# A macaron layer with routed experts on one core: dispatching two tiles at a time, with the norm's inverse deviation computed on the vector engine

## The reference

```python
x = x + 0.5 * ffn(layernorm(x))
x = x + attention(layernorm(x))          # linear attention, 16 heads of 8, phi = silu + 1
x = x + 0.5 * ffn(layernorm(x))          # the same weights as the first

def layernorm(x): return (x - mean(x)) / sqrt(var(x) + 1e-5)

def ffn(x):                              # 128 -> 256 -> 128
    shared = (silu(x @ sg.T) * (x @ su.T)) @ sd.T
    probs = sigmoid(x @ router.T + bias) # 8 experts
    scores, indices = top_k(probs, 2)    # of equal ones the lower index
    scores = scores / sum(scores)
    routed = sum over the two picks of
             score * ((silu(x @ gate[e].T) * (x @ up[e].T)) @ down[e].T)
    return shared + routed
```

## Time and profile before

| | us |
|---|---|
| median of three runs | 1146.66 (1145.6 to 1148.42) |
| the profiled execution | 1145.73 |
| its span | 1144.0 |
| POOL busy | 661.0 (58%) |
| PE busy | 779.2 (68%) |
| DVE busy | 628.9 (55%) |
| ACT busy | 483.5 (42%) |

### The profile page before, as it was taken

One profiled execution on the slowest core, in us unless ns is written; L12 is line 12 of the kernel. 1 busy time (PEld: TensorE's weight loads), 2 busy tenths in 40 slices (PEclk: granted clock), 3 DMA queues, 4 the chain that ended last, 5 costly groups with the idle time before them and its releaser, 6 DMA issues.

```text
span 1144.0 us, 18271 instructions
## 1 busy us (share of the span) xinstructions
PE 779.2 (68%) x5188; PEld 699.2 (61%) x5188; DVE 628.9 (55%) x2120; ACT 483.5 (42%) x871; POOL 661.0 (58%) x713
## 2 busy tenths in 40 slices
PE   4666667568787887637667676775638888888830
PEld 3545545458787877536566554564538787788820
DVE  5666667634444444346766776776734444444435
ACT  3434333145555555334444433333216555555510
POOL 2777777725555555525655477777734555555530
PEclk9877787779999999958989988779769989999965
DMA  8121111222222222131120011111122222222249
GB/s 262 49 62 60 50 43 45 66 78 82 79 84 78 80 75 78 54 113 56 60 69 2 6 46 44 45 45 43 47 87 72 81 80 75 82 75 78 78 146 320
DMA packets 61777, 87.94 MB, mean 77 GB/s; under 512 B 12848, under 2 KB 43568, under 8 KB 61680
## 3 DMA queue, kind: packets, MB, share of 16 engines
q1 hardware_dynamic: 44400, 51.09, 15.2%
q0 software_dynamic: 17280, 35.69, 9.6%
HBM read 43.82 MB, written 42.91 MB: 76 GB/s over the span
## 4 chain that ended last, share of the span: by engine, by line
PE 34%; POOL 21%; issue 16%; DVE 13%; another core or an unknown queue 4%; DMA 4%; ACT 3%; SPq 2%; ACTq 1%; DVEq 0%; POOLq 0%
POOL x_rows L408 14%; PE y_bank L699 10%; PE g_bank L592 4%; PE u_bank L594 4%; POOL rstd L373 3%; PE g_bank L594 3%; PE u_bank L593 3%; PE g_bank L593 3%; PE u_bank L592 3%; DMA y_in<-y_rows 3%; POOL phi_k L427 2%; PE u_bank L744 2%; PE route_bank L674 1%; PE tr_bank L674 1%
## 5 line engine op out<-in xcount | busy, mean ns | idle before, releaser
L420 POOL DMA_INDIRECT y_rows<-y_out,y_to x284 | 272.4, 959 | 243.8 <-DVE y_out L1029 153.2
L408 POOL DMA_INDIRECT x_rows<-send,send_to x256 | 249.6, 975 | 97.3 <-issue 72.7
L1019 DVE TENSOR_TENSOR h<-silu_g,u_bank 128x512 f32<-128x512 f32 x142 | 97.6, 687 | 194.5 <-ACT silu_g L527 91.7
L699 PE MATMUL y_bank<-w_dn,h 128*128 x1136 | 164.1, 291 | 27.5 <-DVE h L1019 26.0
L699 PEld LDWEIGHTS y_bank<-w_dn,h 128*128 128x128 f32 x1136 | 151.0, 206 | 32.5 <-issue 32.3
L513 ACT ACTIVATE slot_gu<-w_gu 128x1024 fp32r x142 | 150.3, 1058 | 40.7 <-issue 29.7
L467 ACT ACTIVATE xn<-x,shift,rstd 128x128 f32<-128x128 f32 x192 | 79.1, 482 | 177.0 <-DVE shift L803 177.0
L600 PE MATMUL tr_bank<-ident,xn 128*128 128x128 f32 x192 | 44.2, 373 | 134.6 <-ACT xn L467 133.3
L592 PE MATMUL g_bank<-xT_hi,slot_gu 128*128 128x256 f32 x284 | 95.2, 335 | 53.0 <-DVE xT_lo L1010 40.4
L600 PEld LDWEIGHTS tr_bank<-ident,xn 128*128 128x128 f32 x192 | 29.8, 187 | 140.1 <-ACT xn L467 109.2
L592 PEld LDWEIGHTS g_bank<-xT_hi,slot_gu 128*128 128x128 f32 x284 | 57.0, 201 | 61.6 <-DVE xT_lo L1010 48.8
(11 more groups left out here) (159 smaller groups left out, 1941.4 us busy)
## 6 DMA issues: line engine op xcount, KB each, us to landing
rows<-x_rows SPq DMA_DIRECT2D x142, 130.0 KB
y_in<-y_rows SPq DMA_DIRECT2D x32, 512.0 KB, 4.1
y_rows<-y_out,y_to POOLq DMA_INDIRECT x284
x<-x_in SPq DMA_DIRECT2D x16, 256.0 KB, 7.3
x_rows<-send,send_to POOLq DMA_INDIRECT x256
out<-x SPq DMA_DIRECT2D x16, 256.0 KB, 3.5
w_raw<-w_experts SPq DMA_DIRECT2D x9, 256.0 KB
x_rows<-pad SPq DMA_DIRECT2D x16, 130.0 KB
```

The costliest lines, as they stand in the source:

```text
L408: pool.indirect_dma_start(x_rows, bass.IndirectOffsetOnAxis(ap=send_to[par][:, w, j:j + 1], axis=0), send[par][:, w, j, :], None).then_inc ...
L420: pool.indirect_dma_start(y_rows, bass.IndirectOffsetOnAxis(ap=y_to[k][:, j:j + 1], axis=0), y_out[k][:, j, :], None).then_inc(y_sent[k], 16)
L699: last = pe.matmul(y_bank[par][:, j * P:(j + 1) * P], h[par][0][:, c * ROWS + j * P:c * ROWS + (j + 1) * P], w_dn[:, bass.ds(e, 1), c, :]. ...
L1019: dve.tensor_tensor(h[par][0][:], silu_g[par][:], u_bank[par][:], ALU.mult).then_inc(slot_h_done, 1)
```

## The change

The 16 tiles are dispatched in groups: (0), (1), (2, 3), (4, 5), ... (14, 15).

```diff
+SEND_RING = 4
+BATCHES = ((0,), (1,), (2, 3), (4, 5), (6, 7), (8, 9), (10, 11), (12, 13), (14, 15))
-ROW_RING = 6
+ROW_RING = 8
+DEEP = 3
+LOGITS_READ, SAFE_STEP, MASK_STEP, WEIGHT_STEP = 1, 4, 18, 21
+NORM_STEPS = 15
```

```diff
 # POOL
-            norm_scale(0, 0)
-            norm_scale(1, 1)
...
             def ffn_tile(f, t):
-                r = f * tiles + t
-                par = t % 2
-                if t + 2 < tiles:
-                    norm_scale((FFN2 if f else FFN1) + t + 2, par)
-                pool.wait_ge(route_step, (r + 1) * ROUTE_STEPS)
-                pool.wait_ge(send_done, r + 1)
+                b = BATCH_OF[t]
+                i = t - BATCHES[b][0]
+                pool.wait_ge(route_step, (batch_no(f, b) + 1) * ROUTE_STEPS)
+                pool.wait_ge(row_tail_done, f * tiles + t + 1)
+                pool.wait_ge(send_copied, f * tiles + t + 1)
                 for w in range(PICKS):
                     for j in range(SUB):
+                        k = i * SUB + j
                         pool.indirect_dma_start(
-                            x_rows, bass.IndirectOffsetOnAxis(ap=send_to[par][:, w, j:j + 1], axis=0),
-                            send[par][:, w, j, :], None).then_inc(sent[par], 16)
-                if f == 0 and 1 <= t < EXPERTS:
-                    split_low(t)
```

```diff
 # ACT
+            def send_normalised(f, t):
+                b = BATCH_OF[t]
+                i = (t - BATCHES[b][0]) * SUB
+                act.wait_ge(norm_step, (batch_no(f, b) + 1) * NORM_STEPS)
+                wait_count(act, sent[t % SEND_RING], sent_count(f, t - SEND_RING))
+                for j in range(SUB):
+                    k = i + j
+                    last = act.activation(send[t % SEND_RING][:, 0, j, 0:P], x_sub(t, j), ACT.Identity,
+                                          bias=ffn_shift[b % 2][:, k:k + 1], scale=ffn_rstd[b % 2][:, k:k + 1])
+                last.then_inc(send_xn_done, 1)
+            def send_second(f, t):
+                k = t % SEND_RING
+                act.wait_ge(send_xn_done, f * tiles + t + 1)
+                act.activation(send[k][:, 1, :, 0:P], send[k][:, 0, :, 0:P], ACT.Copy).then_inc(send_copied, 1)
+            def route_silu(f, b):
+                n = len(BATCHES[b]) * SUB * ROUTED
+                act.wait_ge(route_step, batch_no(f, b) * ROUTE_STEPS + SAFE_STEP)
+                act.activation(z_silu[:, 0:n], z_safe[:, 0:n], ACT.Silu).then_inc(z_silu_done, 1)
+            def dispatch(f):
+                for t in BATCHES[0]:
+                    send_normalised(f, t)
+                for b, ts in enumerate(BATCHES):
+                    for t in ts:
+                        xT_high(m_tile(f, t))
+                        if f == 0 and t == 0:
+                            split_high(0)
+                        send_second(f, t)
+                    route_silu(f, b)
+                    for t in ts:
+                        for c in range(HALVES):
+                            silu(f * tiles + t, c)
+                        if f == 0 and 1 <= t < EXPERTS:
+                            split_high(t)
+                        if f == 0 and t == tiles - 3:
+                            act.wait_ge(attn_loaded, 64)
+                            act.activation(attn_hi[:], attn_raw[:, 0:3 * P], ACT.Copy).then_inc(split_hi, 1)
+                    if b + 1 < len(BATCHES):
+                        for t in BATCHES[b + 1]:
+                            send_normalised(f, t)
```

```diff
 # PE
+            def dispatch(f):
+                for b, ts in enumerate(BATCHES):
+                    for t in ts:
+                        transpose_ffn(f, t)
+                    if f == 0 and b == 0:
+                        pe.wait_ge(split_lo, SPLIT_ROUTER)
+                    for t in ts:
+                        router(f, t)
+                    if f == 0 and b == 0:
+                        pe.wait_ge(split_lo, split_expert(0))
+                        pe.wait_ge(consts_ready, 2)
+                    for t in ts:
+                        n = f * tiles + t
+                        gate_up(n, 0, t % 2)
+                        if t == ts[0]:
+                            ranks(f, b)
+                        gate_up(n, 1, t % 2)
+                        if t > 0:
+                            down_shared(f, t - 1)
+                down_shared(f, tiles - 1)
```

```diff
 # DVE
+            def norm(f, b):
+                ts = BATCHES[b]
+                n = len(ts) * SUB
+                base = batch_no(f, b) * NORM_STEPS
+                for i, t in enumerate(ts):
+                    if f == 0 and t in x_waits:
+                        dve.wait_ge(*x_waits[t])
+                    for j in range(SUB):
+                        op = dve.bn_stats(stats[:, i * SUB + j, :], x_sub(t, j))
+                op.then_inc(norm_step, 1)
+                rstd_, shift_ = ffn_rstd[b % 2][:, 0:n], ffn_shift[b % 2][:, 0:n]
+                var_, half, y, yy = var[:, 0:n], minus_half_var[:, 0:n], guess[:, 0:n], square[:, 0:n]
+                for step in range(1, NORM_STEPS):
+                    dve.wait_ge(norm_step, base + step)
+                    if step == 1:
+                        for k in range(n):
+                            op = dve.bn_aggr(means[:, k, :], stats[:, k, :])
+                    if step == 2:
+                        op = dve.tensor_scalar(var_, means[:, 0:n, 1], EPS, None, ALU.add)
+                    if step == 3:
+                        op = dve.tensor_scalar(half, var_, -0.5, None, ALU.mult)
+                    if step == 4:
+                        op = dve.tensor_scalar(y.bitcast(I32), var_.bitcast(I32), -0.5, RSQRT_MAGIC, ALU.mult, ALU.add)
+                    if step in (5, 8, 11):
+                        op = dve.tensor_tensor(yy, y, y, ALU.mult)
+                    if step in (6, 9, 12):
+                        op = dve.tensor_tensor(yy, yy, half, ALU.mult)
+                    if step in (7, 10):
+                        op = dve.scalar_tensor_tensor(out=y, in0=yy, scalar=1.5, in1=y, op0=ALU.add, op1=ALU.mult)
+                    if step == 13:
+                        wait_count(dve, send_xn_done, f * tiles + (BATCHES[b - 2][-1] + 1 if b > 1 else 0))
+                        op = dve.scalar_tensor_tensor(out=rstd_, in0=yy, scalar=1.5, in1=y, op0=ALU.add, op1=ALU.mult)
+                    if step == 14:
+                        op = dve.scalar_tensor_tensor(out=shift_, in0=means[:, 0:n, 0], scalar=-1.0, in1=rstd_,
+                                                      op0=ALU.mult, op1=ALU.mult)
+                    op.then_inc(norm_step, 1)
...
 # route: steps 6 to 17 of 25
+                    if step in (6, 12):
+                        op = dve.tensor_reduce(score[:, step // 12, 0:n], grid((prob, rest)[step // 12]), AX_X, ALU.max)
+                    if step in (7, 13):
+                        op = dve.tensor_tensor(grid(best), grid((prob, rest)[step // 12]), wide(score[:, step // 12]),
+                                               ALU.is_equal)
+                    if step in (8, 14):
+                        op = dve.tensor_tensor(grid(best), grid(best), by_expert(falling), ALU.mult)
+                    if step in (9, 15):
+                        op = dve.tensor_reduce(first_best[:, 0:n], grid(best), AX_X, ALU.max)
+                    if step in (10, 16):
+                        op = dve.tensor_tensor(pick[:, step // 16, 0:n], grid(best), wide(first_best), ALU.is_equal)
...
+            def dispatch(f):
+                norm(f, 0)
+                for b, ts in enumerate(BATCHES):
+                    for t in ts:
+                        xT_low(m_tile(f, t))
+                        if f == 0 and t == 0:
+                            split_low(0)
+                    route(f, b, 0, MASK_STEP)
+                    multiply(f * tiles + ts[0], 0)
+                    route(f, b, MASK_STEP, ROUTE_STEPS)
+                    row_tails(f, b)
+                    if b + 1 < len(BATCHES):
+                        norm(f, b + 1)
+                    else:
+                        slot_table(f)
+                    for t in ts:
+                        if t > ts[0]:
+                            multiply(f * tiles + t, 0)
+                        multiply(f * tiles + t, 1)
+                        if t > 0:
+                            add_shared(f, t - 1)
...
```

```diff
                 slot_transpose(f, 0)
+                slot_transpose(f, 1)
                 for s in range(slots):
-                    if s + 1 < slots:
-                        slot_transpose(f, s + 1)
+                    if s + 2 < slots:
+                        slot_transpose(f, s + 2)
                     slot_gate_up(f, s)
-                    if s > 0:
-                        slot_down(f, s - 1)
+                    if s > 1:
+                        slot_down(f, s - 2)
+                slot_down(f, slots - 2)
                 slot_down(f, slots - 1)
```

585 lines of the change are left out of this document (247 added, 338 removed).

## The result

The changed kernel takes 1314.2 us (median of four runs, 1306.33 to 1322.06) against 1146.53, a ratio of 1.146 (95% interval 1.1385 to 1.1535). The profiled execution took 1311.02 us with a span of 1309.0, 165.0 more than before.

| stretch | before | after | difference |
|---|---|---|---|
| start to first scatter | 28.8 | 24.7 | -4.1 |
| first dispatch, first to last scatter | 199.7 | 279.1 | +79.4 |
| to the first slot's scatter | 18.9 | 15.7 | -3.2 |
| slot stage | 238.8 | 239.7 | +0.9 |
| to the second dispatch | 168.0 | 169.7 | +1.7 |

The account below looks back on a forecast made before the run. POOL's scatters set the dispatch pace and hold back PE's completions. From 1145.7 us profiled, +75 and +96 for the dispatches and -24 for the slots gave 1292.7, set as 1290; range 1090 to 1340, likeliest case 1225 to 1340.

Parts of the forecast that it names:

- the likeliest case: Whole kernel: PE's completions are withheld during runs of 16 scatters; chance 0.57, own range 1225 to 1340 us.
- Withheld completions: Dispatches: while POOL issues scatters back to back, PE's later results are released only 1.3 to 1.9 us after the run.
- The count of 21 to 28 matmuls: Dispatches: PE's results come late after some 21 to 28 matmuls since the run of scatters began.
- The round of 35 us: Full dispatch rounds of two tiles: 20.2 us of scatters, then release, parts, transposes, router, routing and tails; 35 us.
- The groups of one: First rounds of a dispatch: a group of one tile takes some 18 us.
- The dispatches: Both dispatches: 275 us each from first to last scatter, +75 in the first and +86 in the second.
- The second dispatch's start: Before the second dispatch: first tile's norm and transposes now follow the attention's last addition, first scatter +10 us.
- The slots: Both slot stages: third buffers let PE run one slot further ahead; -12 us per stage taken, range -28 to 0.
- the burst that grows from three slots to four: Slot stages: one more slot in flight between releases, from 3.48 to 3.08 us per slot, 28 us less per stage.
- The 40.4 us of PE and 47.5 of DVE: Both slot stages: PE's waits for xT_lo before the gate product and DVE's remote waits before h, cited for the faster case.
- The chain-bound case: Rival: prompt completions, but groups take 28.3 us at half the clock; total 1194 us, chance 0.13.
- The faster case: Rival: prompt completions, groups of 24.5 us, slots gain 40 us each; total 1089 us (1040 to 1130), chance 0.26.

Follow-up runs that it names:

- e1: Changed kernel plus a POOL wait, between a group's two tiles, for the first tile's down product to be signalled; 1205.22 us, 1.0498 of the kernel before.
- e3: Kernel before plus 24 idle matmuls of 8 columns in front of the first gate product; 1219.09 us, ratio 1.0619.
- e9: Changed kernel with 16 groups of one tile instead of two and seven of two; 1282.55 us, 1.1189 of the kernel before.
- e7: Kernel before with one of the two result scatters of each slot left out; slot stages of 176.2 and 176.3 us.
- e8: Changed kernel with one of the two result scatters of each slot left out; slot stages of 174.2 and 174.1 us.
- e4: Kernel before plus 8 idle matmuls of 256 columns in front of the first gate product; 1165.4 us, ratio 1.0151.
- e2: Changed kernel plus two POOL additions of 256 columns between the scatters of a group's two tiles; 1243.02 us, 1.0827 of the kernel before.

## Why the prediction was right

**The forecast**, 1290 us with 1225 to 1340, held 1314.2, a rise of 168 us where 143 was forecast, and the likeliest case is the one that happened. Part of it is luck, as the steps show:

*Withheld completions.* Right in kind, as e1, e3 and the semaphores' times show. The count of 21 to 28 matmuls, from which I took it that the transposes would be held, fits this kernel and the one before but not e1 and e9. And one step was too simple: I let nothing out before the end of a run. In the twelve full rounds the first tile's down product was due 8 to 10 us into the run, and its addition began inside the run each time, at 13.4 to 19.9 us, 3 to 12 us late. The transposes of the first tile came out after the run's end in eight rounds (21.2 to 22.7 us from its start) and inside it in four (16.3 to 18.4). In those four the transposes of the second tile, due near the run's end, were late again by 1.7 to 3.0 us, so that the round gained only 2 to 4 us. So there are moments inside a run at which something gets out; what sets them is open.

*The round of 35 us.* Measured in the twelve: 33.3 to 38.2, mean 36.3. Its terms: release, in the eight rounds, 0.8 to 2.8 us after the run's end instead of 1.7; and from the first high part to the routing 7.5 us (192.80 to 200.31 in the round shown) where my terms give 4.6 to 5.9. Both routers stand there, at half the clock, 2.57 us each for twelve products, and I had charged one, from full to half. The granted clock of the first dispatch fell from 0.80 to 0.69, with PE idle for up to 12.8 us in a round; but e9's second dispatch has 0.68 without late signals, so the new order lowers it by itself. The groups of one took 17.2 (18 forecast, though the terms that I listed for it add up to 21.3), the first pair behind them 22.8 (27): there the run has 8 scatters, and the transposes came prompt, which I had charged with the release.

*The dispatches.* 275 forecast, 279.1 and 281.1 measured; with the start of the first, which came 4.1 earlier where I took none, +75.3 against +75. The second is +91.4 against +86. That the first comes out so exactly is luck: its full rounds were 7 us longer in all and its last run 2, its first two rounds 5 shorter and its start 4 earlier.

*The second dispatch's start.* Its first scatter stands 18.0 us behind the attention's last addition, forecast 17, before 7.5. But I booked the whole of it as +10. The norms and transposes of the second block's first tiles are gone from the attention, and from the last slot scatter to the last addition it takes 151.7 us instead of 160.5. What is left is +1.7. This term was moved, not added.

*The slots.* -12 per stage forecast, +0.9 and +2.0 measured. The step that failed is the burst that grows from three slots to four. That the y, gate and up banks, which still have two buffers, carry the burst, as the prediction said of y_bank, is likely but not tested. e7 and e8 show that the third buffers are worth 2 us of 176 even where nothing is withheld. The 40.4 us of PE and 47.5 of DVE went to late completions and not to too few buffers: with one scatter per slot they are gone without a third buffer. The 3.48 us per slot was too high as well, since the window of 247 us holds the 9 before the first slot's scatter; by the scatters it is 3.36, and the gain of 28 us would have been 20.

These add up to 165 in the span: +75 and +91 for the dispatches, +3 for the slots, +2 for the attention, and -6 between the dispatches and the slots' first scatters, which I had not looked at. The sum of 1292.7 for the profiled execution lies 18 below the 1311.0 measured: the slots were booked 27 too low in all and the second dispatch's length 5, the attention 8 and the stretches in front of the slots 6 too high.

**The rivals.** The chain-bound case (1194) had more in it than the 0.13 that I gave it. It fits e1: with one pause more a round takes 27.1, near its 28.3, and the total is 1205 (the terms listed for that round add up to 23.8 to 26.3, not to 28.3; with 26.3 the case would have stood at 1170). And it is what e9 does, at 1.12 of the kernel before's time and with nothing held in its dispatches. So in groups of two the new order, with completions let out once per 8 scatters, costs some 55 us, and the runs of 16 without a pause 109 more. The faster case would have needed prompt completions in the slots as well; nothing in the change brings them.

**The semaphore tail.** The Trainium skill (TensorE: Matmul & The Clock Gate, The cost: per-tile semaphore tail) has some 26 ns per increment. That does not cover this: the transposes of the round shown above carry one increment, end at 181.5 by the record and are seen at 192.8.

## What to carry to other kernels

Where POOL issues indirect DMAs back to back, look at when the consumers of PE's results start and not at when the matmuls end; a "remote" wait of several us that ends with, or 1 to 2 us after, a run of scatters is the sign. Put a pause into the run, by a wait for the very result that the next stage needs, or keep the POOL work that makes one: a small operation there can be worth more than it costs. With 2.2 us from scatter to scatter the rounds stayed regular; with 1.49 and 1.55 most results came out only in the next run. Then look at the chain by itself: with groups of one nothing was late, and the kernel still took 1283 us. Whoever frees an engine should first ask what its idle time was doing for others.

## What the runs showed of the hardware that was not expected

- PE's signals reach other engines up to 12.8 us late while POOL issues scatters at 1.27 us each, and in the changed kernel 0.8 to 2.8 us after a run of 16 at the latest. DVE's and ACT's signals, 293 in the same runs of scatters, are never later than 0.013 us.
- What decides which signal is held is open. In the kernel before, e3 and e4 the number of matmuls since the run began fits, whether they have 8 or 512 columns: 18 and 23 are in time, 21 within 0.9 us, 29 and more late. In e1 28 and 34 are in time, in e9 33. Neither PE's time nor the time since the run began fits better (e3, e4). No run here tells whether it is the writing of descriptors or the order of semaphore updates; a scatter with less data or a plain DMA from POOL was not tried.
- Whether other work on POOL withholds is open too: in one round of twelve a completion came out 1.3 us after the last scatter while POOL added, in the others 3.1 us or more after it, when scatters were being issued again (e2).
- With half of the scatters a slot stage runs at PE's own pace, 174 of 177 us busy at a granted clock of 1.00 (e7), and no signal of PE is later than 0.015 us; the full one has 0.94.
